# Tokens sorted by expert on the chip, each tile multiplied by its own expert only, in a fused attention and mixture-of-experts layer

## The reference

```python
x = L0_attn_x                                  # (4, 1024, 256), fp32
xn = layernorm(x)                              # over the last axis
# attention: Q, K, V = xn @ W.T reshaped to 16 heads of 16, softmax(Q K^T) V,
# out + xn, then normalised over each batch entry (mean and variance over 1024 x 256)
# experts: 8, top 2, hidden 1024
logits = xn @ w_gate.T
top_logits, top_idx = top_k(logits, 2)
gates = softmax(top_logits) placed at top_idx, 0 elsewhere
for e in range(8):
    y = y + gates[:, e:e+1] * ((xn @ w_in[e].T) @ w_out[e].T)
result = x + attention(xn) + y
```

## Time and profile before

| | us |
|---|---|
| median of 3 runs | 1054.75 |
| lowest, highest | 1052.57, 1057.66 |
| the profiled execution's own time | 1050.42 |
| its span in the trace | 1048.6 |
| PE busy | 1007.0 |
| DVE busy | 875.9 |
| ACT busy | 627.5 |
| POOL busy | 78.4 |

### The profile page before, as it was taken

How to read it: one execution, slowest core, us unless ns; L and a number is a source line. 1 busy time by engine, 2 the same in 40 slices (tenths; PEclk the granted TensorE clock), 3 DMA queues, 4 the chain that set the end, 5 groups by cost and what they waited for, 6 DMA issues and landing times.

```text
span 1048.6 us, 20711 instructions
## 1 busy us (share of the span) xinstructions
PE 1007.0 (96%) x7816; PEld 524.0 (50%) x7816; DVE 875.9 (84%) x1255; ACT 627.5 (60%) x1231; POOL 78.4 (7%) x205
## 2 busy tenths in 40 slices
PE   6698999999999999999999999999999999999995
PEld 6476788888885433333333333333333333333332
DVE  4331678787768999999999999999999999999976
ACT  2120011211110288888888888888888888888885
POOL 2100011001100000000000000000000000010001
PEclk9899999999999899999999999999999999999998
DMA  9588346545555012222222222222222222222204
GB/s 349 212 290 265 101 107 170 151 122 165 145 147 159 5 54 73 60 72 58 72 60 72 60 70 62 70 62 68 64 68 64 63 69 64 68 61 70 61 27 161
DMA packets 127042, 108.58 MB, mean 104 GB/s; under 512 B 81120, under 2 KB 102368, under 8 KB 126944
## 3 DMA queue, kind: packets, MB, share of 16 engines
q1 hardware_dynamic: 114016, 86.03, 28.9%
q10 hardware_dynamic: 12928, 21.24, 6.0%
HBM read 80.75 MB, written 42.21 MB: 117 GB/s over the span
## 4 chain that ended last, share of the span: by engine, by line
PE 89%; DVE 6%; issue 1%; DMA 1%; ACT 1%; ACTq 1%; POOL 0%; SPq 0%; POOLq 0%; DVEq 0%
PE ps L921 27%; PE ps L903 22%; PE ps L856 15%; PE ps L891 11%; PE ps L819 5%; PE ps L792 3%; PE ps L807 2%; PE ps L932 2%; DVE negm L628 1%; PE ps L944 1%; DVE acc L616 1%; PE ps L780 1%; ACTq L443 1%; DVE spare L560 1%; ACT stage L440 1%
## 5 line engine op out<-in xcount | busy, mean ns | idle before, releaser
L628 DVE TENSOR_REDUCE negm<-ps 128x1 f32<-128x1024 f32 x512 | 619.0, 1222 | 30.4 <-PE ps L891 12.1
L472 ACT ACTIVATE wp<-ps 128x512 f32<-128x512 f32 x684 | 369.4, 603 | 87.3 <-PE ps L903 60.1
L903 PE MATMUL ps<-qf,kf 50*128 50x512 f32 x1024 | 388.6, 456 | 1.9 <-DVE ps L696 1.7
L891 PE MATMUL ps<-kf,qf 48*128 48x512 f32 x1024 | 368.2, 450 | 0.2 <-DVE negm L628 0.2
L903 PEld LDWEIGHTS ps<-qf,kf 50*128 50x128 f32 x1024 | 160.0, 186 | 206.4 <-ACT wp L472 107.3
L921 PE MATMUL ps<-wp,vb 128*17 128x256 f32 x2736 | 215.4, 387 | 0.3 <-issue 0.3
L891 PEld LDWEIGHTS ps<-kf,qf 48*128 48x128 f32 x1024 | 145.9, 186 | 7.4 <-issue 5.7
L472 ACT ACTIVATE vstage<-ps 128x512 f32<-128x512 f32 x170 | 102.4, 602 | 24.9 <-PE ps L903 11.2
L856 PE MATMUL ps<-mth,xth 128*128 128x512 f32 x256 | 103.8, 405 | 3.4 <-DVE spare L560 2.5
L921 PEld LDWEIGHTS ps<-wp,vb 128*17 128x17 f32 x2736 | 46.9, 95 | 119.1 <-ACT wp L472 45.9
L472 ACT ACTIVATE picks<-ps 128x512 f32<-128x512 f32 x170 | 102.6, 603 | 0.0
(11 more groups left out here) (106 smaller groups left out, 724.0 us busy)
## 6 DMA issues: line engine op xcount, KB each, us to landing
feat_d<-qk_d SPq DMA_DIRECT2D x64, 256.0 KB, 4.4
qf<-feat_d SPq DMA_DIRECT2D x128, 128.0 KB
qk_d<-stage ACTq DMA_DIRECT2D x32, 256.0 KB
qk_d<-spare ACTq DMA_DIRECT2D x32, 256.0 KB
qf<-feat_d SPq DMA_DIRECT2D x128, 64.0 KB
kf<-feat_d SPq DMA_DIRECT2D x128, 64.0 KB
v_d<-vstage ACTq DMA_DIRECT2D x8, 544.0 KB, 4.9
vb<-v_d SPq DMA_DIRECT2D x128, 34.0 KB, 2.6
```

Source lines behind the costliest of these rows:

```text
L472: nc.scalar.activation(weight_tile(n, j, b)[:, h * HALF:(h + 1) * HALF], ps[:, ST_BANK[(2 * unit + b) % 3], :], ACT.Exp).then_inc(exp_done, 1)
L628: nc.vector.tensor_reduce(negm[:, n % 2, qt:qt + 1], ps[:, b:b + 2, :].rearrange("p b c -> p (b c)"), AX.X, ALU.max, negate=True).then_inc ...
L891: last = nc.tensor.matmul(ps[:, MAX_BANK[turn % 2] + half, :], qf[rows, u, qt * P:(qt + 1) * P], kf[rows, u, :], start=True, stop=True)
L903: nc.tensor.matmul(ps[:, ST_BANK[(2 * unit + half) % 3], :], kf[rows, u, j * P:(j + 1) * P], qf[rows, u, h * HALF:(h + 1) * HALF], start=T ...
```

## The change

The tokens are sorted by expert on the chip in two parts (`PARTS` = 2, 2048 tokens each, which is 4096 choices). A part is padded to 40 tiles (`TILES`), so there are 80 tiles in 20 blocks of four (`NMB`), where each tile belongs to one expert.

- `layernorm` writes `xn` directly; POOL's copy is gone. `xnc` serves as a third pair of weight slots (three slots instead of four), then as buffer for sorted tokens, then for gathered rows. layernorm(1) moves ahead of choose_experts(0), the others are spread over the prelude.
- The projections of chunks 2 to 7 follow the prelude on their own.
- DVE counts choices (`count_choices`), PE sums them with a triangular matrix (`rank_choices`), DVE works out each token's two places, the places of the padding rows and each tile's expert (`start_tiles`, `place_choices`, `place_padding`, `name_owners`): part 0 in the middle of the projections, part 1 after them.
- POOL scatters the rows of `xn` to `xs_d` in DRAM with 32 indirect DMAs a part and 8 for padding.
- SP loads the sorted tokens block by block, PE transposes them, ACT and DVE split them, and `expert_tile` multiplies each tile with its expert in 4 matmuls (two of 512 columns, which hold the high and the low half of M side by side in `mm`, and two of 256); the column is chosen at run time from registers. ACT copies one half, DVE adds the other; SP stores the rows to `ys_d`.
- `max_scores` of groups 0 and 1 come after the last tile of blocks 4 to 19.
- In attention, POOL gathers each token's two rows, weighs them and adds them to `acc`. SP issues 48 of the 64 regroups there, one a group, `AHEAD` = 16 groups ahead.

The diff, cut to its core:

```diff
+    AHEAD = 16
+    PARTS = 2
+    PT = NT // PARTS
+    TILES = -(-((2 * PT * P + E * (P - 1)) // P) // TC) * TC
+    MB = TILES // TC
+    NMB = PARTS * MB
+    WARM = NMB - 2 * NKT
...
+            def sorted_tokens(b):
+                if b >= 2:
+                    sp.wait_ge(xt_psum, KT * (NC + b - 1))
+                if b % MB == 0:
+                    sp.wait_ge(scattered[b // MB], 16 * (2 * PT + E))
+                sp.dma_start(xnc[:, b % 2], xs_d[b // MB][b % MB * CH:(b % MB + 1) * CH].rearrange("(t p) d -> p t d", p=P)).then_inc(xs_in[b % 2], 16)
+
+            def expert_rows(b):
+                sp.wait_ge(moe_added, TC * (b + 1))
+                sp.dma_start(ys_d[b // MB][b % MB * CH:(b % MB + 1) * CH].rearrange("(t p) d -> p t d", p=P), outs[b % 4]).then_inc(ys_out[b % 4], 16)
+
+            sp.wait_ge(m_ready, KT * E)
+            sorted_tokens(0)
+            sorted_tokens(1)
+            for b in range(NMB):
+                if b >= 1 and b + 1 < NMB:
+                    sorted_tokens(b + 1)
+                if b == NMB - 2:
+                    max_rows(0)
+                expert_rows(b)
...
                 max_rows(n + 1)
+                if n + AHEAD < NB:
+                    regroup(n + AHEAD)
...
+            for part in range(PARTS):
+                for k in range(2):
+                    pool.wait_ge(placed, 2 * part + k + 1)
+                    for t in range(PT * part, PT * (part + 1)):
+                        nc.gpsimd.indirect_dma_start(
+                            out=xs_d[part], out_offset=bass.IndirectOffsetOnAxis(ap=placeu[:, k, t:t + 1], axis=0),
+                            in_=xn[:, t, :], in_offset=None).then_inc(scattered[part], 16)
+                pool.wait_ge(att_const, 2)
+                pool.wait_ge(padded, part + 1)
...
+            for n in range(NB):
                 if n % 2 == 0 and n >= 4:
                     residual(n // 2 - 2)
                 max_halves(n)
+                if n % 2:
+                    gather(n // 2)
+                elif n:
+                    combine(n // 2 - 1)
+            combine(NT - 1)
...
             xt_out(2)
             for c in range(2, NC):
                 v_out(c)
+                if c + 1 < NC:
+                    xt_out(c + 1)
+                if c > 2:
+                    second_weight(c - 1)
                 qk_out(c)
...
+            for c in range(2, NC):
+                if c > 2:
+                    choose_experts(c - 1)
+                    count_choices(c - 1)
+                if c + 1 < NC:
+                    lo_halves(c + 1)
+                if c == NC // PARTS:
+                    start_tiles(0)
+                qk_lo_halves(c, range(2))
+                if c == NC // PARTS:
+                    place_choices(0)
+                qk_lo_halves(c, range(2, 4))
+                if c > 2:
+                    gate_weights(c - 1)
+                if c == NC // PARTS + 1:
+                    place_padding(0)
+                    name_owners(0)
+
+            choose_experts(NC - 1)
+            count_choices(NC - 1)
+            gate_weights(NC - 1)
+            start_tiles(1)
+            place_choices(1)
+            place_padding(1)
+            name_owners(1)
+            lo_halves(NC)
...
+            def expert_tile(i, owners):
+
+                p, tokens = (NC + i // TC) % 2, slice(i % TC * P, (i % TC + 1) * P)
+                own = i % TILES
+                e = (owners[own // PACK] >> (3 * (own % PACK))) & (E - 1)
...
+                products = ((xth, 0, 2 * D), (xtl, 0, D), (xtl, 1, D), (xth, 1, 2 * D))
+                for j, (v, kt, columns) in enumerate(products):
+                    last = nc.tensor.matmul(ps[:, Y_BANK[i % 4], 0:columns], v[:, p, kt, tokens],
+                                            m[:, kt, bass.ds(e * (2 * D), columns)], start=j == 0, stop=j == len(products) - 1)
...
             pe.wait_ge(qk_lo, 4 * NC)
             pe.wait_ge(att_const, 2)
+            transposes(NC)
+            for i in range(PARTS * TILES):
+                if i % TILES == 0:
+                    owners = owner_words(i // TILES)
+                expert_tile(i, owners)
+                if i % TC == 0 and i + TC < PARTS * TILES:
+                    transposes(NC + i // TC + 1)
+                if i % TC == TC - 1 and i // TC >= WARM:
+                    n, qt = divmod(i // TC - WARM, NKT)
```

403 lines of the change are left out of this document (251 added, 152 removed).

## The result

| | kernel before | changed kernel | forecast |
|---|---|---|---|
| median, us | 1054.4 | 1215.1 (1213.4 to 1216.3) | 1112 (1055 to 1160) |
| ratio | 1 | 1.152, interval 1.149 to 1.155 | 1.055 |
| profiled span, us | 1048.6 | 1213.8 | 1105 |

The change costs 161 us where 57 were forecast. Two of the twelve runs of one later kernel, the one with the split in the first four groups, were slow ones (1055.9 and 1085.95 us) and are left out of its median and ratio. The profile page of the changed kernel shows busy times, the slices of PE and of its granted clock, the chain's shares by engine and by line, and the groups of the expert stage's transposes and of the score products (rows of before: the earlier trace rows).

What follows compares the result with a forecast made beforehand. It took TensorE, busy for 96% of the span, as the bound, and attention's start as deciding. +54.5 us there and +2 in attention make +57: span 1105, run 1107, plus 4.3 to the median, 1112 us (1055 to 1160).

Steps and rivals of the forecast that it cites:

- Prelude: Forming expert products M: earlier layernorm(1) removes a TensorE wait; last product ends at 93.6 instead of 104.8 us, gain 11.2.
- Projection stage: Projections of chunks 2 to 7 with nothing beside them, plus part 0's small sorting steps on VectorE: ends at 182 us.
- The 13.0 us a chunk: Projection stage: project_v, copies, casts, subtractions and DMA issues take 13.0 us a chunk, against 9.5 of TensorE work.
- Indirect DMAs: Part 0's 40 scatters on POOL, between 135 and 195 us: 1.3 us each, just fitting; part 1's hidden beside part 0.
- the rival sum of 80 us: Part 0's scatters at about 2 us fixed each, paid serially: 80 us, expert stage some 22 us late; no separate chance.
- the forecast's cases: Whole-kernel outcomes: quick loop or hidden load 12%, loop with upper clock 20%, forecast 48%, slower at 1130 to 1170 us 20%.
- Serial tail: After the projections, about 61 small VectorE steps, 13.6 us, plus lo_halves 1.4; expert stage then starts at 197 us.
- Expert stage: Sorted-token products: a store, load, compute loop of 11.4 us for 18 blocks plus 10 us, 215 us; attention starts at 412.
- the allowance of 2.0 us for the clock: Each expert block: 2.0 us added to 9.4 for transposes and tiles at the lower clock; bounds 0 and 3.0.
- The two rivals in which the loop closed quickly or the clock held: Expert stage: 7.5 us a block, about 1040 us (12% with hidden load, 980); or 9.4, 1065 to 1080 us (20%).
- Attention: Attention stage: gathers and combining hidden on POOL; small row loads meeting a regroup add 2 us, bounds -1 and +8.
- Direction: Whole kernel: slower 85%, within 0.5% 4%, faster by over 0.5% 11%.

Runs made afterwards that it cites:

- the one with the split in the first four groups: Changed kernel plus load of block b+2 ahead, gathers at even groups' start, query and key-half feature loads split for four groups: 1045.5 us, 0.989 of the kernel before.
- the split alone: Changed kernel with only the features' two-copy and key-half loads split in two, for all groups: 1140.4 us, 27 us below the changed kernel.
- the combined version: Changed kernel plus load of block b+2 ahead, gathers at even groups' start and features' loads split in all groups: 1035.3 us, 0.979 of the kernel before.

## Why the prediction was wrong, point by point

All times are starts or ends read in the traces; "again" is the changed kernel without steps.

| | forecast | changed | again |
|---|---|---|---|
| last product M ends near | 93.6 | 93 | 94 |
| last projection subtracted | 182 | 239 | 228 |
| expert stage starts | 197 | 254 | 244 |
| expert stage, length | 215 | 246 | 215 |
| attention starts | 412 | 501 | 459 |
| attention and end, against before | +2 | +22 | +16 |

- **Prelude: right.** 93 to 94 us, the gain of 11 us.
- **Projection stage: the step that failed.** The 13.0 us a chunk was the engines' own time, and as such it was right: with the scatters held back and the features moved the stage ends at 189 us. A chunk's casts and subtractions also wait for the landing of the stores of the chunk before. The sum puts this wait at nothing and gives no reason, and it leaves out that the stage runs beside two streams which make the landing late. The first is the features' loads, which in the kernel before ran at 104 to 121 us too, but under 28 us of PE work with no store of a projection: 20.6 us. The second is the scatters, of which I asked only whether they would be in time: 37.2 us in three waits. The stage ends 46 us late: 7 by the sum itself and 39 by these two. The waits add up to more, 57.8 us; taken out one after the other, the features gave 23 us (228 to 205) and the scatters 16 (205 to 189). The granted clock of the stage is 0.78 with the waits and 0.89 without them, so part of the 39 us may be the clock. Of what the all-expert product had covered I named the ACT and DVE chain and left out the DMAs.
- **Indirect DMAs: right in price, wrong in effect.** They are 1.27 us apart, against 1.3 taken. The fixed 2 us each of the Trainium skill ("DMA: Bandwidth & Descriptors", "Anatomy of one DMA — SWDGE (gpsimd) path") is not paid one after the other, so the rival sum of 80 us is void. (Its own delay was also given as 22 us where 135 and 80 make 215, 18 past 197.) None of the forecast's cases had a hand-over from PE to ACT that comes only every 10 us while POOL issues its DMAs; these steps are 48 us of the 161. Without them the time, 1167 us, is still past the forecast's 1160.
- **Serial tail: right.** 15 to 16 us against 15.0 (61 small steps and lo_halves).
- **Expert stage: right.** 215 us again. Eighteen times the last addition of a block comes 11.3 us after that of the block before on average (10.4 to 12.4), where I had 18 times 11.4 and 10 us around them. Landing 4.7 us (4.8 taken), transposes 1.97 at the lower clock, clock 0.74 to 0.75. Three tiles took 2.7 to 3.9 us, between 2.17 and twice that, so the allowance of 2.0 us for the clock was near. The rule of the Trainium skill ("TensorE: Matmul & The Clock Gate", "HAM oscillation — how this bites in real kernels") holds for the transposes, and for the products only in part. With the load ahead the stage is 105.5 us, and in the combined version its clock is 0.94. The two rivals in which the loop closed quickly or the clock held are excluded.
- **Attention: mis-sized, mechanism half right.** I took +2 us, bounds -1 and +8, for row loads that meet a regroup. The row loads are indeed what became late, but through the gathers, and only together with the two-engine form of the features' loads: 16 us again, 5 with the split alone (696.1 against 690.7), and two groups at 21.1 us without the gathers too, with all regroups still there. That POOL's time for the gathers is hidden was right.
- **Direction** and its chance of 85% were right. The miss of 103 us is 46 (projection), 14 (attention) and 48 (steps), less 5, nearly all of it the 4.3 us that the forecast had added to come from the profiled run to the median.

The cause of the steps is not settled. Shown: the same program has them on one occasion and chip and not on another (48 us); where they occurred, plain DMAs from the same queue did not have them. Not shown: what holds PE's updates for 10 us, and whether the plain form would be free of them each time, since each was run once there.

**The version that beats both.** Sorting with the load two blocks ahead, the gathers at the start of even groups and the features' loads split: 1035.3 us, 2.1% (1.6 to 2.7) below the kernel before and 11% below the changed kernel again. The gain of sorting is thus real: attention starts at 335 us instead of 358. It had been covered by one line of queue order (110 us again), by the form of the features' loads (27 us) and, where they occur, by the steps. Most of what is left is the scatters beside the projections' stores, up to 24 us.

## What to carry to other kernels

When a change takes away a long stretch of TensorE work, list not only the engines but also every DMA that ran under it, and ask who now waits for its landing. Before a transfer is moved, look at its rate: if it moves a fixed low GB/s with the engines' share near 0.1, its form may have too few engines; three moves here only carried 20 to 36 us along, and the split removed them. And run the base once more beside the experiments: a 48 us effect that came and went with the occasion made three runs look like proofs of things that they did not test, and it cannot be told here from an effect of the chip.

## What I had not expected of the hardware

- The same program at 1215 us (four runs, 1213.4 to 1216.3) and at 1167 us (two runs), with the kernel before within 3 us beside both. In the slower case PE's semaphore updates reach ACT one per 10 us or so while indirect DMAs are being issued 1.27 us apart, and most of the updates of these DMAs are missing from the trace.
- While the features' loads with a slowest dimension of 2 are what moves, the rate is 51 to 58 GB/s, and with them and the gathers in flight a small load of two rows takes 4.3 us to land instead of 2.0. The completion updates in a trace (3, 9 or 16 a DMA) tell such forms apart.
- Indirect scatters of 128 KB at 1.27 us each lengthen the landing of plain stores of 256 KB so much that waits of 11 to 15 us come of it; the plain form of the same bytes does the same (15.3 and 11.8 us).
